# Inverse softmax sums turned by a 32x32 block transpose, a masked spread and two row-tiled products with a constant, where widened rows were turned by full tile transposes

## What is computed

```python
latent_kv = x @ w_kv_down
kv = latent_kv @ w_kv_up
k, v = (kv[..., :HD], kv[..., HD:])
q = (x @ w_q).reshape(Bx, Tx, N_HEAD, HEAD_SIZE)          # 16 heads of 64
att = jnp.einsum('bqhd,bkhd->bhqk', q, k) * scale
att = jnp.where(causal, att, -jnp.inf)
att = jax.nn.softmax(att, axis=-1)
y = jnp.einsum('bhqk,bkhd->bqhd', att, v)
return y.reshape(Bx, Tx, HD) @ w_out
```

## Time and profile before

| | |
|---|---|
| time, median of 3 runs | 1823.37 us (1819.48 to 1824.26) |
| the profiled execution: its own time | 1825.55 us |
| its span, from the first to the last instruction | 1824.1 us |
| granted TensorE clock, mean | 0.994 |
| PE busy | 1735.6 us (95%) |
| DVE busy | 1257.9 us (69%) |
| ACT busy | 891.2 us (49%) |
| POOL busy | 854.1 us (47%) |
| instances of the turn: transposes on PE | 256, of 273 ns in the record each |
| widening copies on POOL | 256, of 289 ns each |

### The profile page before, as it was taken

One profiled execution on the slowest core, in us unless ns is written; L12 is line 12 of the kernel. 1 busy time (PEld: TensorE's weight loads), 2 busy tenths in 40 slices (PEclk: granted clock), 3 DMA queues, 4 the chain that ended last, 5 costly groups with the idle time before them and its releaser, 6 DMA issues.

```text
span 1824.1 us, 39951 instructions
## 1 busy us (share of the span) xinstructions
PE 1735.6 (95%) x15734; PEld 1203.2 (66%) x15734; DVE 1257.9 (69%) x2775; ACT 891.2 (49%) x1970; POOL 854.1 (47%) x1282
## 2 busy tenths in 40 slices
PE   7899999998999999999899999999989999999998
PEld 4566675767566667566856667756775666766667
DVE  5688857626688884762678887575367888676445
ACT  5577725233467662422456775332246677443233
POOL 2677743141177784232127777324113777731420
PEclk9899999999999999999999999999999999999999
DMA  8555560141155554031125555305013555520500
GB/s 235 120 135 131 117 186 1 24 71 37 53 131 126 131 125 156 1 62 32 37 80 128 134 121 122 136 2 93 1 40 98 130 130 125 134 103 2 93 1 25
DMA packets 120185, 164.45 MB, mean 90 GB/s; under 512 B 30304, under 2 KB 87104, under 8 KB 118976
## 3 DMA queue, kind: packets, MB, share of 16 engines
q1 hardware_dynamic: 106560, 155.62, 35.5%
q10 hardware_dynamic: 13440, 6.30, 1.2%
HBM read 63.22 MB, written 4.24 MB: 37 GB/s over the span
## 4 chain that ended last, share of the span: by engine, by line
PE 76%; DVE 10%; SPq 7%; ACT 3%; DMA 2%; issue 1%; POOL 1%; DVEq 0%; ACTq 0%; POOLq 0%
PE bank L653 11%; PE scores L451 11%; PE scores L633 9%; PE bank L451 7%; PE bank L694 5%; SPq L970 4%; DVE prob L784 3%; PE scores L1717 2%; PE scores L1630 2%; PE bank L700 2%; PE scores L1084 2%; SPq L348 2%; DMA placed<-prob 2%; PE bank L696 2%; PE scores L422 2%; PE scores L1153 2%
## 5 line engine op out<-in xcount | busy, mean ns | idle before, releaser
L853 POOL COPY placed<-prob 32x768 f32<-32x768 f32 x384 | 315.4, 821 | 27.5
L288 POOL TENSOR_TENSOR rstd<-rstd,minus_half 128x2 f32<-128x2 f32 x96 | 69.9, 729 | 542.1 <-DVE rstd L287 541.5
L653 PEld LDWEIGHTS bank<-placed,v_t 128*64 128x64 f32 x4608 | 252.3, 138 | 87.7 <-issue 87.7
L653 PE MATMUL bank<-placed,v_t 128*64 128x128 f32 x4608 | 275.1, 276 | 20.1 <-DMA placed<-prob 15.1
L633 PE MATMUL scores<-k_t,q_t 64*128 64x512 f32 (+3 forms) x1536 | 274.8, 497 | 0.2
L777 DVE CUSTOM_DVE_ANT_0 mod_rows<-scores,hx 128x128 f32<-128x128 f32 (+7 forms) x256 | 191.8, 749 | 79.5 <-PE scores L633 79.5
L784 DVE STREAM_TRANSPOSE prob<-prob 128x1536 f32<-128x1536 f32 x128 | 223.2, 1766 | 24.3 <-ACT prob L895 24.1
L777 DVE CUSTOM_DVE_ANT_0 x<-scores,hx 128x128 f32<-128x128 f32 (+7 forms) x256 | 192.6, 752 | 0.0
L895 ACT ACTIVATE prob<-mod_rows,neg_max 128x128 f32<-128x128 f32 (+2 forms) x192 | 137.3, 715 | 99.6 <-DVE neg_max L777 79.6
L633 PEld LDWEIGHTS scores<-k_t,q_t 64*128 64x128 f32 x1536 | 129.7, 187 | 84.1 <-issue 61.9
L841 POOL COPY rec_wide<-rec 128x128 f32<-128x128 f32 x256 | 65.0, 289 | 239.9 <-DVE rec L788 178.4
(11 more groups left out here) (261 smaller groups left out, 3363.4 us busy)
## 6 DMA issues: line engine op xcount, KB each, us to landing
placed<-prob SPq DMA_DIRECT2D x640, 96.0 KB, 2.2
f<-in_L_ffn_f SPq DMA_DIRECT2D x16, 2048.0 KB, 13.4
placed<-hx SPq DMA_DIRECT2D x320, 96.0 KB, 2.2
mod_rows<-mod_scratch SPq DMA_DIRECT2D x32, 128.0 KB, 4.5
out<-x SPq DMA_DIRECT2D x16, 256.0 KB, 2.2
x<-in_L_attn_x SPq DMA_DIRECT2D x6, 512.0 KB, 4.4
w_ring<-in_L_attn_w_q ACTq DMA_DIRECT2D x24, 128.0 KB, 2.5
w_ring<-in_L_attn_w_kv_up ACTq DMA_DIRECT2D x48, 64.0 KB, 2.0
```

The costliest lines, as they stand in the source:

```text
L288: step = pool.do(lambda e, ts=ts: nc.gpsimd.tensor_tensor(rstd[:, ts], rstd[:, ts], minus_half[:, ts], op=ALU.pow), var, filled)
L653: last = nc.tensor.matmul(out_bank[rows_, at_:at_ + P], v_t[pair % 2][:, j, rows_], placed[m % 2][:, :, head, first_block(m, i) + j, :], s ...
L853: nc.gpsimd.tensor_copy(placed[m % 2][target * GROUP:(target + 1) * GROUP, source, :, :, :], prob[m % 3][source * GROUP:(source + 1) * GRO ...
```

## The change

The inverse sums take another way from `row_sum` to `rec_t`:

- DVE `invert`: the reciprocal goes to `inv_cols` (128x32, the rest zero), and after a wait for it a 32x32 block transpose gives `inv_rows`: token within a group of 32 in the columns, the sum's index in the partitions. For m > 0 the transpose also waits for `widened` of the round before.
- POOL `widen`: one multiplication instead of one copy for each tile. It spreads `inv_rows` over tiles and groups of 32 tokens and multiplies by a 0/1 mask, so that each partition keeps only what belongs to it: `inv_wide`, 128 x (tiles x 64).
- PE `turn_inverse`: two products instead of four or two transposes. Partitions 0 to 63 hold half of the tokens, 64 to 127 the other half. The constant `head_wide` (1 where a partition's sum is of this head) is the weight, `inv_wide` streams. One product writes to the third bank of `score_tiles[0]`, the other to that of `score_tiles[1]`.
- ACT `copy_rec`: two copies, one from each bank, instead of one.
- The list of last readers of the banks now has `rec_copied` for the third bank of `score_tiles[0]` too.
- Once: masks are made at the start (three small DVE operations, one memset), and at each batch's start POOL writes `head_wide`.

```diff
@@ the layout of the list of last readers, for the steps behind the loop
-        banks.readers = [all_of("values_read"), all_of("job_read_act")] + [all_of("masked")] * 5 + [all_of("rec_copied")]
+        banks.readers = [all_of("values_read"), all_of("job_read_act")] + [all_of("masked"), all_of("masked"), all_of("rec_copied")] * 2
@@ PE
-        rec_bank = score_tiles[1][:, SCORE_BANKS - 1, :]
+        rec_banks = [s[:, SCORE_BANKS - 1, :] for s in score_tiles]
             def turn_inverse(m):
+                if m == 0:
+                    e.wait_ge(flow["head_ready"], b + 1)
...
-                for k in range(len(tiles_in(m))):
-                    last = nc.tensor.transpose(rec_bank[:, k * P:(k + 1) * P], rec_wide[:, k, :], ident[:, :])
+                count = len(tiles_in(m))
+                for r, rows_ in enumerate(ROWS_OF):
+                    last = nc.tensor.matmul(rec_banks[r][:, 0:count * HD0], head_wide[rows_, :, :].rearrange("p h d -> p (h d)"),
+                                            inv_wide[rows_, 0:count, :, :].rearrange("p s g i -> p (s g i)"), start=True, stop=True)
@@ DVE
             def invert(m):
-                k, count = column_of(m, 0, 0), HEADS * len(tiles_in(m))
-                nc.vector.reciprocal(rec[:, k:k + count], row_sum[:, k:k + count]).then_inc(flow["inverted"], 1)
+                k, count = (m % 2) * 8, HEADS * len(tiles_in(m))
+                nc.vector.reciprocal(inv_cols[:, 0:count], row_sum[:, k:k + count]).then_inc(flow["inverted"], 1)
+                e.wait_ge(flow["inverted"], base["inverted"] + m + 1)
+                if m > 0:
+                    e.wait_ge(flow["widened"], base["widened"] + m)
+                nc.vector.transpose(inv_rows[:, :], inv_cols[:, :]).then_inc(flow["inverse_turned"], 1)
@@ POOL
             def widen(m):
...
-                for i, tile in enumerate(tiles_in(m)):
-                    at_ = k + HEADS * i
-                    last = nc.gpsimd.tensor_copy(rec_wide[:, out_slot(m, tile), :].rearrange("p (a n) -> p a n", a=HEADS),
-                                                 rec[:, at_:at_ + HEADS].unsqueeze(2).to_broadcast([P, HEADS, HD0]))
+                last = nc.gpsimd.tensor_tensor(
+                    inv_wide[:, 0:count, :, :], inv_rows[:, :].unsqueeze(1).unsqueeze(1).to_broadcast([P, count, 2, 32]),
+                    inv_mask[:, :, 0:count].rearrange("p g s -> p s g").unsqueeze(3).to_broadcast([P, count, 2, 32]), op=ALU.mult)
@@ ACT
-                nc.scalar.copy(rec_t[m % 2][:, 0:cols], rec_bank[:, 0:cols]).then_inc(flow["rec_copied"], 1)
+                by_part = rec_t[m % 2][:, 0:cols].rearrange("p (s r n) -> p r s n", r=2, n=HD0)
+                for r in range(2):
+                    last = nc.scalar.copy(by_part[:, r, :, :], rec_banks[r][:, 0:cols // 2].rearrange("p (s n) -> p s n", n=HD0))
+                last.then_inc(flow["rec_copied"], 1)
```

More of the change, by code:

```diff
@@ L156, in build @@
     rec = sb("rec", [P, HEADS1])
+    inv_cols, inv_rows = sb("inv_cols", [P, 32]), sb("inv_rows", [P, 32])
+    inv_mask, head_of = sb("inv_mask", [P, 2, 4]), sb("head_of", [P, 2])
     logit_max = sb("logit_max", [P, G])
@@ L194, in build @@
     flow = {k: semaphore(k) for k in (
-        "scores_done", "masked", "exp_done", "shuffled", "values_read", "kept", "moved_even", "moved_odd", "values_done", "inverted", "widened",
+        "scores_done", "masked", "exp_done", "shuffled", "values_read", "kept", "moved_even", "moved_odd", "values_done", "inverted",
+        "inverse_turned", "head_ready", "widened",
         "rec_turned", "rec_copied", "normed", "job_done", "job_read_dve", "job_read_act",
@@ L317, in build @@
     minus_halves = fill(minus_half[:, :], -0.5)
+    inv_cleared = fill(inv_cols[:, :], 0.0)
     select(tril[:, :], [[1, P]], 0, -1, ALU.is_ge, 0.0, fill(tril[:, :], 1.0))
@@ L478, in batch @@
         rec_t = [part("rec_t", [P, 4 * P]), tmp[:, 0:2, :].rearrange("p t n -> p (t n)")]
-        rec_wide = part("rec_wide", [P, 4, P])
+        inv_wide = part("inv_wide", [P, 4, 2, 32])
+        head_wide = part("head_wide", [P, 2, HD0])
         wq_dram = I["L0_attn_w_q"].rearrange("(c p) n -> p c n", p=P)
@@ L534, in batch @@
                      "shuffled": HEADS * ROUNDS, "kept": len(COPIES) * ROUNDS, "values_done": ROUNDS, "inverted": ROUNDS,
-                     "widened": ROUNDS, "rec_turned": ROUNDS, "rec_copied": ROUNDS, "values_read": ROUNDS, "normed": ROUNDS,
+                     "inverse_turned": ROUNDS, "widened": ROUNDS, "rec_turned": ROUNDS, "rec_copied": ROUNDS, "values_read": ROUNDS, "normed": ROUNDS,
                      "job_done": len(JOBS) * PAIRS, "job_read_dve": 2,
@@ L765, in column_of @@
         def column_of(m, i, head):
-            return (m % 2) * 8 + i * HEADS + head
+            return (m % 2) * 8 + out_slot(m, tiles_in(m)[i]) * HEADS + head
         def dve_pairs(e):
@@ L834, in widen @@
             def widen(m):
-                k, count = column_of(m, 0, 0), len(tiles_in(m))
-                e.wait_ge(flow["inverted"], base["inverted"] + m + 1)
+                count = len(tiles_in(m))
+                e.wait_ge(flow["inverse_turned"], base["inverse_turned"] + m + 1)
                 if m > 0:
                     e.wait_ge(flow["rec_turned"], base["rec_turned"] + m)
-                for i, tile in enumerate(tiles_in(m)):
-                    at_ = k + HEADS * i
-                    last = nc.gpsimd.tensor_copy(rec_wide[:, out_slot(m, tile), :].rearrange("p (a n) -> p a n", a=HEADS),
-                                                 rec[:, at_:at_ + HEADS].unsqueeze(2).to_broadcast([P, HEADS, HD0]))
+                last = nc.gpsimd.tensor_tensor(
+                    inv_wide[:, 0:count, :, :], inv_rows[:, :].unsqueeze(1).unsqueeze(1).to_broadcast([P, count, 2, 32]),
+                    inv_mask[:, :, 0:count].rearrange("p g s -> p s g").unsqueeze(3).to_broadcast([P, count, 2, 32]), op=ALU.mult)
                 last.then_inc(flow["widened"], 1)
@@ L864, in norm @@
                 last.then_inc(flow["normed"], 1)
+            e.wait_ge(flow["masked"], base["masked"] + 1)
+            nc.gpsimd.tensor_copy(head_wide[:, :, :], head_of[:, :].unsqueeze(2).to_broadcast([P, HEADS, HD0])
+                                  ).then_inc(flow["head_ready"], 1)
             for m in range(ROUNDS):
@@ L979, in batch @@
                       for k in ("job_read_dve", "job_read_act", "normed", "exp_done", "kept")]
-        first_weights = []
+        first_weights, masks_folded = [], []
         if b == 0:
@@ L992, in batch @@
                                                      axis=AX_X, op=ALU.add), masks_done)
+            dve.do(lambda e: nc.vector.tensor_reduce(head_of[:, :], ident[:, :].rearrange("p (q h) -> p h q", h=2),
+                                                     axis=AX_X, op=ALU.add))
+            turned_groups = ident[:, :].rearrange("p (r g c) -> p r g c", r=2, g=2)[:, :, :, 0:8]
+            by_column = inv_rows[:, 0:16].rearrange("p (g c) -> p g c", g=2)
+            folded = dve.do(lambda e: nc.vector.tensor_tensor(by_column, turned_groups[:, 0, :, :], turned_groups[:, 1, :, :],
+                                                              op=ALU.add))
+            masks_folded.append(dve.do(lambda e: nc.vector.tensor_reduce(
+                inv_mask[:, :, :], by_column.rearrange("p g (s h) -> p g s h", h=2), axis=AX_X, op=ALU.add), folded))
         sp.do(sp_pairs)
         pe.do(pe_pairs, *before_pairs, *lat_done)
-        dve.do(dve_pairs, future_done)
+        dve.do(dve_pairs, future_done, inv_cleared)
         act.do(act_pairs)
         act.do(lambda e: nc.scalar.activation(spare_column[:, :], minus_half[:, 0:1], ACT.Gelu_apprx_tanh))
-        pool.do(pool_pairs)
+        pool.do(pool_pairs, *masks_folded)
         def all_of(name):
```

## The result

| | before | changed |
|---|---|---|
| median, first measurement | 1822.32 us (6 runs) | 1830.65 us (1829.32 to 1831.45, 6 runs) |
| median, second measurement, another chip | 1823.51 us (25 runs) | 1829.99 us (1825.31 to 1833.58, 8 runs) |
| ratio | | 1.0043 (1.0029 to 1.0057); again 1.0033 (1.0021 to 1.0046) |
| profiled execution | 1825.55 us, span 1824.1 | 1831.02 us, span 1829.8 |
| PE, DVE, ACT, POOL busy | 1735.6, 1257.9, 891.2, 854.1 us | 1739.3, 1278.9, 898.9, 836.4 us |

The account below looks back on a forecast made before the run. PE was taken to bound the kernel, with 76% of the chain. Steady part 0, starts 0.5 and tails 3.8 gave 4.3 us more: 1829.9 us on the profiled time, 1827.7 on the median; range 1820.5 to 1835.5.

Parts of the forecast that it names:

- slower by over 0.3%: Whole kernel: the outcome that the time rises beyond 0.3%, from 1828.9 us; chance 0.34.
- within: Whole kernel: the outcome that the time stays within 0.3% (5.5 us) of before; chance 0.55.
- own range of the forecast: Whole kernel: the forecast as worked out, 1825.3 to 1830.5 us, for late transfers falling otherwise; chance 0.50.
- Steady part, 0: PE's steady rounds: streaming costs the same, the shape change moves ahead of the turn; 0, bounds 8 us either side.
- on both sides: Rival at PE's turns: array shape change lost before and behind the turn, 8 us on top, 1835.5 us; chance 0.16.
- cheaper ahead: Rival at PE's turns: shape change ahead costs nothing in all 88, -3.7 us in sum, 1819.7 us; chance 0.12.
- the product at half the rate: Rival on PE: the turn's product streams at half the scores' rate, 28 us more, 1855.8 us; chance 0.02.
- The price of a change of shape, 0.09 us: PE between 128-row and 64-row products: each change of array shape loses 0.09 us.
- The tail, 3.8 us: Each batch's tail: tile 5's products wait for ACT's copies, plus a shape change; 0.94 us in four batches, bounds 2.8 to 4.8.
- The starts, 0.5 us: Starts of batches 1 and 2: DVE's added wait and transpose delay round 1's minimum 0.25 us each; bounds 0.3 to 1.0.
- ACT and POOL, 0: ACT's extra copy time is covered before scores' third bank, POOL's work is off the chain; no cost or gain.

Follow-up runs that it names:

- experiment 6: Changed kernel with each turn's pair of products issued twice to the same banks: 1850.3 us, ratio to the kernel before 1.0150.
- experiment 5: Changed kernel with the turn moved between a round's two projection products: 1860.9 us, ratio to the kernel before 1.0205.
- experiment 1: Kernel before with one line changed: rec_copied also listed as last reader of the third bank of scores0: 1828.97 us, ratio 1.0032.
- experiment 3: Changed kernel with two banks exchanged in the ring, so tile 5's products use a bank the turn doesn't write: 1827.79 us, ratio to before 1.0028.
- Experiment 2: Kernel before with DVE's wait for the reciprocal and an unused 128x32 block transpose added in every round: 1824.67 us, ratio 1.0007.
- experiment 7: Kernel before with ACT's copy of the turned inverses made in two halves: 1823.62 us, ratio 0.9994.
- experiment 4: Changed kernel with each batch's last turn moved on PE ahead of the seven products for tile 3: 1827.38 us, ratio to before 1.0026.
- experiment 8: Changed kernel with the last turn early, DVE's inverse work among the next round's minima, POOL's spread between its copies: 1829.99 us, ratio to before 1.0035.
- experiment 10: Kernel before with DVE's added wait and unused block transpose in rounds 0 and 1 of each batch alone: 1824.59 us, ratio 1.0005.
- experiment 11: Kernel before with DVE's added wait and unused block transpose in rounds 2 to 23 alone: 1824.66 us, ratio 1.0013.

## Why the prediction was right, and where it was off

The measured 1830.65 us lies within 1820.5 to 1835.5, slower as forecast, but 3 us above the 1827.7 and beyond 0.3% of the time before: of my cases, "slower by over 0.3%" (0.34) came true, not "within" (0.55). The own range of the forecast ended at 1830.5, just short of it; the wide range held it thanks to the room kept for rivals that the runs refute. The direction and the place of the loss were right by reasoning; that the time fell inside was in part luck.

- **Steady part, 0.** Right, and its two halves also. The pair streams as the scores do (experiment 6), and the change of shape moves from behind the turn to ahead of it (3.21 for 3.23 us). The rivals "on both sides" and "cheaper ahead" are refuted by the same rows; the product at half the rate by experiment 6. (The first of these is 1827.7 + 8 = 1835.7 us, not 1835.5; nothing hangs on it.) One of the 22 turns of a batch stands behind values and so should save a change of shape. Only 0.04 us of this is seen, since PE's weights for it start 0.07 us behind the end of DVE's last minimum (1120.78 to 1120.85).
- **The price of a change of shape, 0.09 us.** Mis-sized: 0.20 us (experiment 5). I read it from the hole in the earlier trace rows alone. The first pass behind it is slower by another 0.1 us, which the chain's 2.79 for scores held all along. In the steady part this cancels, in the tail it doesn't. The Trainium skill's rule (TensorEngine Tiling (Array Packing), Key Properties), that a change of tiling mode drains the engine, fits what is seen here, with 0.20 us as the price between 128-row and 64-row products. The Trainium skill's advice to turn with transposes rather than products (Perfetto Trace Analysis, Transposes) stands column for column: a pair of products took 0.22 us for 128 columns, a transpose 0.11. The pair costs what the transposes cost (0.43 for 0.44 us) only because it moves half the columns.
- **The tail, 3.8 us.** Right in mechanism, mis-sized: 5.0 us. 0.25 and not 0.09 us around `turn_inverse(22)`; 1.00 and not 0.85 around the last turn. ACT's copies took 0.43 us, for 0.50 forecast; they started 0.53 us behind the turn's start, for 0.42, and the first products behind the hole gave away 0.1. Experiments 1 and 3 show wait and shape apart: the wait alone 0.73 us, the shapes 0.65. Together they are 1.25 and not 1.38: the change of shape behind the last turn (0.2) falls into the wait, while the two copies are 0.06 longer than the one (0.43 for 0.37).
- **The starts, 0.5 us.** The DVE delay came as forecast: 0.25 us more from shuffle to minimum, at every batch start but batch 0's. What it costs cannot be told from the traces' transfer waits. Experiment 2 bounds DVE's whole part to 4 us (ratio up to 1.0022), and its median says 0.7.
- **ACT and POOL, 0.** Right (ACT by experiment 7; POOL is 18 us less busy, and no gain is seen).
- **A term that the sum lacked: the granted clock.** Besides the first and the last microseconds of the program, the clock falls to half for 3.4 or 6.8 us at two kinds of places, the sparse stretch of layer 1's feed-forward and the start of a batch's attention. The second kind was seen only in kernels with DVE's added work in the first rounds: 16 falls at 27 batch starts in nine traces (batches 1 to 3 of the changed kernel twice, of experiments 2, 3, 4, 5, 6, 8 and 10; experiment 3 had none), and none at 12 starts in the four traces without it (before, experiments 1, 7, 11). PE waits there for the minima of round 1, and DVE's 0.25 us lengthen this wait, from 1.67 to 1.92 us. In experiment 5 PE waits 2.79 us, and each of its three starts has a fall. The windows of 10 us at these starts in the changed kernel show the clock below 1, the same stretch of before (from 942.60) does not:

```profile
950.00:960.00 10.00, 8.08 (x36) 3.62 (x34) 9.77 (x20) 6.05 (x13) 6.75 (x9) 0.83 0.48 116
1395.00:1405.00 10.00, 8.08 (x32) 3.75 (x32) 9.80 (x14) 7.15 (x16) 5.55 (x7) 0.91 0.37 95
```

```profile
942.60:952.60 10.00, 7.66 (x48) 3.52 (x46) 9.84 (x18) 6.34 (x14) 7.43 (x14) 1.00 0.52 119
```

(The columns are the stretch, its length, busy time of PE, its loads, DVE, ACT and POOL, the granted clock, then the transfers.) What it cost there, the changed kernel and then before:

```profile
954.77 0.70 PE L672 MATMUL scores<-inv_wide,head_wide 64*128 64x256 f32 x4 [1.92 <-DVE neg_max L786]
955.28 4.47 PE L638 MATMUL scores<-k_t,q_t 64*128 64x512 f32 x16
```

```profile
947.26 0.63 PE L664 MATMUL scores<-ident,rec_wide 128*128 128x128 f32 x4 [1.67 <-DVE neg_max L777]
947.82 3.20 PE L633 MATMUL scores<-k_t,q_t 64*128 64x512 f32 x16
951.61 2.84 PE L653 MATMUL bank<-placed,v_t 128*64 128x128 f32 x48 [0.60 <-DMA placed<-prob]
```

The 16 passes of scores took 4.47 us for 3.20. Before, the values behind them waited 0.60 us for a transfer; now that wait is gone, and from the start of the scores to the values it is 4.39 us (955.28 to 959.67) for 3.79. Half of the 1.27 us was taken in.

How much of the difference of medians (8.3 and 6.5 us, for 5.0 in the tails) is clock? Before at mean clock 0.998 takes 1818.6 us (5 runs), at 0.993 1825.8 (14), at 0.992 1829.1 (4). At 0.993, the changed kernel takes 1830.5 us (10 runs), 4.7 us more. That this is near the 5.0 of the tails proves nothing, because equal mean clock is not equal falls. Two falls of 3.4 us at batch starts lower the mean by 0.0019, all of the 0.0017 that the changed kernel lacks (0.9933 over 14 executions for 0.9950), and a fall there costs less than one in the feed-forward (0.6 us in the rows above, for 1.5). Experiment 10 has the same low mean, 0.9935, without any change in the tail, and loses 1.1 us by the median; its three executions at 0.993 take 1823.8 us, 2 less than before at that mean. So DVE's delay with its falls is worth about 1 us, and its interval allows up to 3.5.

That the DVE delay causes the falls at the batch starts is supported by where they occur. That the clock makes up the rest of the medians is not shown. With 5.0 us of tails and about 1 of starts, 0.5 to 2.3 us stay open. So do 2.1 us of experiment 1, which has no DVE work and no fall at a batch start in its trace (mean clock 0.9943), and the 1 to 2 us of experiment 11.

No version of the changed kernel beat the kernel before. The best is experiment 4.

## What to carry to other kernels

When a helper writes to a second bank, look up who takes that bank next in every stage, the tail included: one entry in a list of last readers costs 0.73 us in each tail here, and the changed work of the steady rounds nothing. When small products change the array's shape, count the changes in the order of the program and price them by the whole groups on both sides, not by the hole. Work that is hidden behind an engine with a wait is hidden only at that place; moved by two instructions, it can be on the path.

## What was not expected of the hardware

- A change between products of 128 rows and of 64 costs 0.20 us of TensorE: 0.09 as a hole and 0.1 in the first pass (experiment 5: 0.40 us for two). The first pass behind a wait is as much slower without any change of shape (experiment 1: 3.29 us for 3.19).
- A 32x32 block transpose of 128x32 takes 212 ns in the record, against 1766 ns for 48 times the columns. With the wait ahead of it, it shifts its follower by 0.25 us.
- The granted clock differs between executions of one program, from 0.992 to 0.998 on average, and the time with it by 10 us of 1824: more than the change in question. The lower clock stood where TensorE had waited (1.92 us at a batch start) or had been sparsely busy (5.8 to 7.0 of the ten microseconds ahead). The same mean clock can go with 2 us less or more, by where the falls lie (experiment 10).
